# A fused RWKV block and NAS-cell attention chain on one core: maxima twelve instead of fourteen steps ahead, and three operations of GpSimd moved

## What is computed

```
for c in range(NUM_NOD):            # 6 nodes
    q = ew[c, 0] * (nodes[in_q] @ We[eq] + be[eq])
    k = ew[c, 1] * (nodes[in_k] @ We[ek] + be[ek])
    v = ew[c, 2] * (nodes[in_v] @ We[ev] + be[ev])
    o = _mha(q, k, v, Wq[c], Wk[c], Wv[c], Wo[c])   # 8 heads of 16, softmax over 1024 keys
    nodes[c] = act_w[c] * o + q
return _layernorm(nodes[5], ln_g, ln_b)
```

## Time and profile before

| | us |
|---|---|
| median of 3 runs | 2336.1 |
| the runs | 2336.1, 2323.18, 2336.68 |
| the profiled execution | 2325.5 |
| its span | 2323.7 |

### The profile page before, as it was taken

One profiled execution on the slowest core, in us unless ns is written; L12 is line 12 of the kernel. 1 busy time (PEld: TensorE's weight loads), 2 busy tenths in 40 slices (PEclk: granted clock), 3 DMA queues, 4 the chain that ended last, 5 costly groups with the idle time before them and its releaser, 6 DMA issues.

```text
span 2323.7 us, 46304 instructions
## 1 busy us (share of the span) xinstructions
PE 2261.4 (97%) x18009; PEld 865.2 (37%) x18009; DVE 2079.0 (89%) x2259; ACT 1827.5 (79%) x3426; POOL 533.9 (23%) x668
## 2 busy tenths in 40 slices
PE   6899999999999999999999999999999999999996
PEld 3534333333333333333333333333333333333332
DVE  7879899999999999998999999999999999999983
ACT  3257888888887888888888888888888888788785
POOL 5331311312203112112112112122022022321302
PEclk9589999999999999999999999999999999999998
DMA  4221313313213223223133133133033132232201
GB/s 117 58 56 39 73 49 78 78 45 79 70 47 87 62 55 82 58 70 78 53 69 78 44 78 78 33 79 89 26 76 82 29 80 71 55 83 53 64 19 51
DMA packets 86522, 149.39 MB, mean 64 GB/s; under 512 B 34315, under 2 KB 48927, under 8 KB 86303
## 3 DMA queue, kind: packets, MB, share of 16 engines
q0 software_dynamic: 28224, 94.13, 18.2%
q1 hardware_dynamic: 58078, 52.30, 8.7%
HBM read 41.97 MB, written 14.91 MB: 24 GB/s over the span
## 4 chain that ended last, share of the span: by engine, by line
PE 54%; DVE 2%; issue 1%; POOL 0%; ACT 0%; POOLq 0%; ACTq 0%; DVEq 0%
PE ring L494 25%; PE context L542 21%; PE ring L464 1%; DVE max_neg L1028 1%; PE ring L436 1%; PE ring L444 1%; PE ring L469 1%; PE ring L455 1%; PE wide L520 1%; DVE max_part L1033 0%; PE ring L340 0%; DVE stats L815 0%; DVE v_aug L923 0%; POOL k_aug L285 0%; POOL ctxT L1147 0%
## 5 line engine op out<-in xcount | busy, mean ns | idle before, releaser
L1028 DVE TENSOR_REDUCE max_neg<-wide 128x1 f32<-128x1024 f32 x1536 | 1842.8, 1219 | 165.9 <-PE wide L520 160.8
L780 ACT ACTIVATE e_ring<-ring 128x512 f32<-128x512 f32 x3072 | 1668.5, 597 | 323.5 <-PE ring L494 196.6
L520 PE MATMUL wide<-k_aug,q_aug 48*128 48x512 f32 x3072 | 1125.4, 449 | 20.5 <-DVE max_neg L1028 11.4
L494 PE MATMUL ring<-q_aug,k_aug 50*128 50x512 f32 x3072 | 1138.4, 448 | 0.0
L542 PE MATMUL context<-e_ring,v_aug 128*32 128x256 f32 (+1 forms) x10752 | 943.3, 423 | 1.4 <-ACT raw L795 1.4
L494 PEld LDWEIGHTS ring<-q_aug,k_aug 50*128 50x128 f32 x3072 | 465.1, 185 | 757.3 <-ACT e_ring L780 552.0
L520 PEld LDWEIGHTS wide<-k_aug,q_aug 48*128 48x128 f32 x3072 | 460.0, 187 | 44.0 <-DVE max_neg L1028 32.4
L542 PEld LDWEIGHTS context<-e_ring,v_aug 128*32 128x32 f32 x10752 | 211.8, 108 | 482.8 <-issue 368.6
L315 POOL DMA_DIRECT2D src<-node_dram x40 | 23.6, 590 | 685.8 <-PE ring L455 685.8
L1129 POOL CAST q_part<-q_part 128x512 fp32r<-128x512 f32 x47 | 29.0, 617 | 435.7 <-ACT q_part L710 435.5
L285 POOL DMA_DIRECT2D q_aug<-q_part x138 | 71.9, 521 | 192.8 <-PE ring L494 192.8
(11 more groups left out here) (213 smaller groups left out, 879.8 us busy)
## 6 DMA issues: line engine op xcount, KB each, us to landing
q_aug<-q_part POOLq DMA_DIRECT2D x138, 256.0 KB, 3.7
k_aug<-k_part POOLq DMA_DIRECT2D x138, 256.0 KB, 7.1
src<-node_dram POOLq DMA_DIRECT2D x40, 512.0 KB, 5.2
ctxT<-raw SPq DMA_DIRECT2D x384, 32.0 KB, 2.0
rden_bc<-rden_dram SPq DMA_DIRECT2D x23, 512.0 KB
node_dram<-node_ring SPq DMA_DIRECT2D x16, 512.0 KB, 2.7
q_aug<-rows_dram SPq DMA_DIRECT2D x192, 8.0 KB
node_ring<-in_L_attn_x SPq DMA_DIRECT2D x4, 512.0 KB, 4.8
```

What stands on the lines that cost most here:

```text
L494: e.matmul(bk[:, :], k_aug[first:first + AUG, u % 2, h // 2, chunk * P:(chunk + 1) * P].bitcast(F32R), q_aug[first:first + AUG, u % 2, h / ...
L520: done = e.matmul(wide[w % 2][:, half_of(kh)], q_aug[first:first + SPLIT, u % 2, h // 2, q0:q0 + P].bitcast(F32R), k_aug[first:first + SPL ...
L780: e.activation(e_ring[:, n % E_SLOTS, :], bank[where["st", n]][:, :], ACT.Exp, scale=EXP_SCALE).then_inc(a_exp, 1)
L1028: e.tensor_reduce(max_neg[:, G % 2, row:row + 1], wide[w % 2][:, :], AX_X, ALU.max, negate=True).then_inc(v_mx, 1)
```

## The change

The lookahead goes from 14 to 12 steps, so the group ends come at r = 4, 12, 20 and 28. What stood at steps -14 and -13 is moved to -12, and most of the rest of that stretch by one step. The turns before it start at `START = -LOOKAHEAD - TURNS`, so they keep their distance from the first maxima. `normalise` moves from r = 11, behind k's six moves, to r = 9, ahead of the second split of k, and no longer waits for `v_neg`. In `affine` the second of three operations now waits for the `max_turn` of r = 28 (in the two units where it starts at r = 26), and the store of the result goes from r = 30 to 31.

```diff
-LOOKAHEAD = 14
+LOOKAHEAD = 12
...
-        FOLDS_AT, BIASES_AT, VALUES0_AT, ONES_AT = (-13, -12, -10, -8, -7), -5, (-4, -3), 4
+        FOLDS_AT, BIASES_AT, VALUES0_AT, ONES_AT = (-12, -11, -9, -7, -6), -5, (-4, -3), 4
...
-            turns_then_steps((7, 7, 8, 17, 17, 17, 17, 17, 18, 21, 24, 24, 28, 29, 30, 30, 31, 31, 32), (-14, -13, -12, -12, -9)),
+            turns_then_steps((7, 7, 8, 17, 17, 17, 17, 17, 18, 21, 24, 24, 28, 29, 30, 30, 31, 31, 32), (-12, -12, -11, -11, -8)),
...
-                             (-13, -12, -11, -10, -9, -9, -7, -6, -5, -5, -1)),
-            (-9, -8, -8, -4, -4, -4, -4, -4, 1, 2, 3, 3, 4, 5, 6, 7, 8, 10, 11, 12, 13, 14, 14, 17),
+                             (-12, -11, -10, -9, -8, -8, -6, -6, -5, -5, -1)),
+            (-8, -7, -7, -4, -4, -4, -4, -4, 1, 2, 3, 3, 4, 5, 6, 7, 8, 10, 11, 12, 13, 14, 14, 17),
...
             if u + 1 < LAST:
-                return (19, 22), (20, 23), (21, 24), 26, 30
+                return (19, 22), (20, 23), (21, 24), 26, 31
...
                 e.wait_ge(d_rden_in, DMA * (u + 1))
-                e.wait_ge(v_neg, (u + 1) * GPU + 3)
                 after()
                 signal(e.tensor_tensor(ctxT[:, :], ctxT[:, :], rden_bc[:, :], ALU.mult), g_norm)
...
                 step(e.tensor_tensor(y3, y3, g3, ALU.mult))
+                if u + 1 < LAST:
+                    e.wait_ge(v_neg, (u + 2) * GPU + 1)
                 after()
                 step(e.tensor_tensor(y3, y3, b3, ALU.add))
...
+                if 0 <= prev < LAST and (r, half) == (KH_AT[1], 1):
+                    normalise(prev)
                 if 1 <= nxt < UNITS and half == 1:
                     if r in KH_AT:
                         split_k(nxt, KH_AT.index(r))
...
                 if 0 <= prev < LAST:
-                    if half == 0 and r == 11:
-                        normalise(prev)
```

## The result

The kernel became slower: 2436.58 us median of 4 runs (2430.87 to 2444.11), against 2333.36 us of before (4 runs, 2323.18 to 2336.68). The ratio is 1.0433, 95% interval 1.0400 to 1.0465. The forecast was 2328.1 us with a range up to 2341; the time lies 96 us above that range. The profiled execution took 2430.87 us, 105.4 more than the one of before.

The account below looks back on a forecast made before the run. TensorE and VectorE's reduces were taken to run side by side, 0.01 us apart. From 2325.5 us profiled, -4.8 + 0 + 1.1 - 2.6 - 0.7 - 1.0 = -8.0 gave 2317.5; carried over to the median, 2328.1, range 2310 to 2341.

Parts of the forecast that it names:

- The rows in time: Rows of `q_aug`, stored four steps ahead of their scores instead of six, would land with 3.6 us to spare.
- POOL's order: In steady units `normalise` at r = 9 takes 2.40 us; k's subtraction ends over a microsecond before r = 12's group end.
- What a stop costs: TensorE stops at r = 3 and 11 were priced at their length, 0.42 us each, 0.84 us a unit.
- a rival whose mechanism was another (group ends at 0.62): Group ends without a product before them stop TensorE 0.62 us instead of 0.23: 35.9 us more, 2364.0; chance 0.06.
- the one that group ends cost nothing: VectorE catches up by itself after group ends, 21.2 us less, 2306.9; chance 0.07.
- The start: Two steps of maxima alone go from before the first scores: -4.8 us, bounds 2.3 and 7.6 of gain.
- the rival by which the start gives nothing: Packed steps before the first scores wait for VectorE or POOL as long as the removed ones took: 2332.9; chance 0.09.
- The clock of the start: Rival: the shifted start changes TensorE's stretches at 1.2 GHz, giving 2316.4 or 2339.8; chance 0.16, half to each side.
- The end: The 14 closing steps of scores alone become 12, but half steps stay 1.23 us long: 0 us.
- Group ends: At r = 4, 12, 20, 28, undisturbed, 0.23 us each: +1.1 us over 14 steady units; L1033 some 16 us in total.
- Units 20 and 22: Scaling a batch's last node no longer meets r = 26's group end: -2.6 us for both units, bounds 0 and -4.
- Unit 9: With `normalise` ahead of k's moves, the 0.7 us by which r = 13 was longer than elsewhere goes: -0.7 us.

## Why the prediction was wrong

The lookahead and the move of `normalise` interact. Medians in us, each with the final scaling as noted (with a lookahead of 14 its first operation waits, with 12 the second):

| | normalise at r = 11, with its wait | normalise at r = 9 |
|---|---|---|
| lookahead 14 | 2333 (before), 2318.3 with the new scaling | 2321.6, 2314.0 with the new scaling |
| lookahead 12, new scaling | 2327.7 | 2436.6 (after) |

Point by point:

- **The rows in time: the step that failed.** The prediction took "the slowest place, behind k's moves" from the earlier trace rows as 3.87 us. In before that store (1258.42) left together with the first move of k, issued from 1258.39, not behind the moves. Behind the moves it takes 7.9 us, behind moves and `src` 8.2 to 9.9, and free 1.95. And "2.0 us to land" was the median of `ctxT` transfers; in unit 12 of after, where the store once more left with the first move and took 3.89, this is the term that was off: the chain has 8.77. With 3.89 + 9.6 the rows take 13.5 us, against the 11.9 - 1.1 = 10.8 allowed: 2.7 late, where 3.1 was measured and 3.6 to spare forecast. I asked how late the row was, and not what else was under way when it would be sent.
- **POOL's order: a second step that failed.** "k's subtraction at r = 11 at the latest" rested on `normalise` taking 2.40 us from its place on. Its wait for the broadcast was priced at nothing, since no trace of before showed one. It takes 7.1 us, and it was hidden only because POOL came late. That set k's subtraction onto the group end of r = 12 and the moves onto the store. It could have been bounded: in before's unit 12 k's cast starts 4.5 us after the broadcast's issue (1255.87 and 1251.38), and before's page has medians of 2.7 us (`node_dram`) and 5.2 (`src`) for other transfers of 512 KB; with the 2.4 us of `normalise` behind it even the shorter one makes k's split late. But this step is not what made the rows late: with the earlier reciprocals POOL kept the order that the prediction had, and 63 of the 103 us stayed.
- **What a stop costs.** I priced every stop at its length. In after 55.1 us of the loss are TensorE's matmuls at the lower clock, more than the stops themselves (52.0). Of the 206.1 us at the lower level 119.5 stand behind stops; the start and the end have 10 us less than in before's execution.
- **The chance.** Late rows had 2 in 100, without a price, inside a rival whose mechanism was another (group ends at 0.62). That rival is out, and with it the one that group ends cost nothing: undisturbed ones cost 0.23 to 0.24.
- **The start** was right: from the first maxima to the first scores 48.9 us instead of 53.0, -4.1 for -4.8. So the rival by which the start gives nothing is out.
- **The clock of the start** was not moved by the change. The stretch at the lower level around the first scores lasts 13.7 us in both profiled executions. The next one lasts 10.2 in before's and 3.4 in after's, but also 3.4 with before's own start (the final scaling alone) and 10.2 with after's (the lookahead without the move of `normalise`), so it differs from one execution to the next.
- **The end** was right: from the first scores of unit 23 to the end 112.0 us instead of 111.9.
- **Group ends** were right where they are undisturbed (the one of r = 4 in unit 12, TensorE: scores 1281.30, maxima 1281.54, 0.24 for 0.23), wrong at r = 12. L1033 takes 27.3 us for 16 forecast.
- **Units 20 and 22** were right in kind: r = 27 takes 2.46 instead of 4.32 us. The 11 us between the profiled execution and the median, which I could not explain, were in this term: with the final scaling held behind the group end the runs lie within 4.4 us, and the profiled one at their median. What the two stops trigger in some executions is worth more than the 2.6 us that I took.
- **Unit 9**: its r = 13 takes 4.92 us, as long as before (4.24 + 0.7). The gain did not come, since the held group end of r = 12 now makes r = 13 as long in the other units too (5.00 in unit 8). With a lookahead of 14 and `normalise` at r = 9 it did come: 4.36 us.
- **The rest of the sum** holds: without the move of `normalise` the kernel took 2327.7 us, where the forecast was 2328.1. That agreement is partly luck, since waits of 8 us and the gain of the scaling cancel in it; against before's runs beside it (2333.25) the gain is 5.6 us, not 8.0. For units 0 to 6 no run gives the term alone: with the transfers out of the way units 1 to 6 take 553.1 us instead of 552.9, where 1.0 less was forecast.

Why `src` alone is over half of the loss in after, when k's moves are three quarters of the bytes, can be read in part. With `src` late the waits fall by 28.8 us (52.0 to 23.2), and TensorE's time at the lower clock from 206.1 to 133.5 us, which is worth 36.3 at half speed; together 65 us, for 64.0 measured. The stops are shorter there, and only 7 of 19 are followed by the lower clock.

Not settled: why the small transfers get no turn until the large ones of the other queue are nearly through. The trace shows that it is so, and no run took the reason apart.

## What to carry to other kernels

When an edit shortens a lead or moves an instruction on a queue, write down, for each small transfer on the path, which large ones will be under way at the moment it is issued, in the new order; the latency that it had in the old order says nothing about that. An instruction that never waited may stand behind its data by luck of its place: look up when the data lands before you move it forward. And two edits that are harmless alone have to be timed together, since each may have used the slack that the other needs.

## What the runs showed of the hardware

- **Small transfers behind large ones.** The 16 KB store of the rows, from SyncE's queue, until its load could be issued: 1.95 us with the engines free, 3.9 us when sent with the first of k's moves (POOL's queue), 7.9 us behind six of them, 8.2 and 9.9 us behind six and `src` (sent 3.0 and 1.4 us after the issue of the last of the six). In unit 12 of after the load fared likewise: issued from 1306.79, it had no packet under way from 1307 to 1313.3, while POOL's queue had 329, and landed at 1316.25 by the chain above. The Trainium skill (DMA: Bandwidth & Descriptors, Queues, rings and completion order) says that each engine takes turns between queues packet by packet, where a packet is some 9 to 17 descriptors as a rule and 64 at most. By that rule the small transfer would have its turn after one packet of the large ones. Here it had none in the 6.9 us in which POOL's queue ran 310 packets as the trace counts them, 19 for each of the 16 engines, and its turn came only near the end of the backlog; whether those are the page's packets or descriptors no run here shows.
- **A transfer that nobody waited for was long.** `rden_bc<-rden_dram`, 512 KB, took 7.1 us from issue to use. q's last move was issued 1.1 us ahead of it, and its packets ran until 1291.96; those of the broadcast ran from 1292.13 to 1296.64, 4.5 us, and POOL started 1.2 us later. After's page has medians of 2.9 us for `node_dram` and 6.4 for `src`, also 512 KB.
- **A short stop can cost twice.** In after, each of the 14 stops of TensorE of 2.3 us or more was followed by 6.8 to 10.2 us at the lower clock, and of five between 0.98 and 2.07 us two were. With `normalise` at r = 11 and no wait, nine stops of TensorE of 0.96 to 2.12 us were followed by 3.4 us of it, and fifteen of 0.93 to 1.22 us by none. In the profiled execution of before with `normalise` at r = 9, three stops of 1.33 to 1.35 us were followed by 10 to 17 us, and one of 1.53 us by none; in before's own, two of 1.36 us by none. So the length of the stop does not decide alone. Such stops make run times spread: a kernel without such stops (the final scaling alone) repeats within 4.4 us.
